# A transformer tower on one core: both feed-forward passes get another split of work between ScalarE, VectorE and GpSimd

## What is computed

```python
h = h + attention(layernorm(h))
x = layernorm(h)                                  # 32 x 257 tokens of 256 values
s = sigmoid(clip_x) * max(abs(x)) / 127           # one scale over all tokens
xq = clip(round(x / s), -128, 127) * s
gate, up = xq @ quant(w_gate).T, xq @ quant(w_up).T          # 704 wide
p = silu(gate) * up
s2 = sigmoid(clip_down) * max(abs(p)) / 127       # again over all tokens
hq = clip(round(p / s2), -128, 127) * s2
out = h + hq @ quant(w_down).T
```

## Time and profile before

| | us |
|---|---|
| median of 3 runs (lowest, highest) | 1266.56 (1261.84, 1271.71) |
| profiled execution, its own time | 1265.48 |
| its span, first to last instruction | 1263.6 |
| embedding, attention and preparation of weights, until about | 985 |
| first pass, first product to last maximum | 998.4 to 1129.3 |
| second pass, to the last residual addition | 1131.5 to 1260.0 |

### The profile page before, as it was taken

How to read it: one execution, slowest core, us unless ns; L and a number is a source line. 1 busy time by engine, 2 the same in 40 slices (tenths; PEclk the granted TensorE clock), 3 DMA queues, 4 the chain that set the end, 5 groups by cost and what they waited for, 6 DMA issues and landing times. The chain is left out here.

```text
span 1263.6 us, 27990 instructions
## 1 busy us (share of the span) xinstructions
PE 996.6 (79%) x9574; PEld 691.5 (55%) x9574; DVE 847.5 (67%) x1907; ACT 675.3 (53%) x1123; POOL 655.9 (52%) x749
## 2 busy tenths in 40 slices
PE   2257989999989998998989988897844577856785
PEld 1135766666766766666767766665633233323332
DVE  1125566677776777677776777665556388888985
ACT  0245655566666666566666666654321366655553
POOL 4235455556565565556555565643321799802333
PEclk9978899999999999999999999998876699987657
DMA  3565554555545655455545655333300144115653
GB/s 108 122 155 137 129 144 119 131 150 144 152 119 138 154 149 133 120 155 142 151 125 137 155 143 142 95 94 103 81 11 1 46 180 172 61 46 187 204 163 125
DMA packets 156710, 158.66 MB, mean 126 GB/s; under 512 B 28360, under 2 KB 152172, under 8 KB 154092
## 3 DMA queue, kind: packets, MB, share of 16 engines
q1 hardware_dynamic: 156652, 157.91, 46.3%
HBM read 70.38 MB, written 31.23 MB: 80 GB/s over the span
## 5 line engine op out<-in xcount | busy, mean ns | idle before, releaser
L518 ACT ACTIVATE prob<-ST 128x772 f32<-128x772 f32 x256 | 209.5, 818 | 165.6 <-PE ST L928 160.9
L683 DVE TENSOR_REDUCE mneg<-SX 128x2 f32<-128x258 f32 x256 | 107.5, 420 | 241.6 <-PE SX L914 241.2
L911 PE MATMUL SX<-kst,qst 96*128 96x257 bf16 (+1 forms) x1024 | 161.8, 252 | 25.5 <-DMA qst<-qpart 15.1
L685 DVE TENSOR_REDUCE mneg<-SX 128x2 f32<-128x514 f32 x256 | 173.9, 679 | 0.0
L928 PE MATMUL ST<-qst,kst 98*128 98x256 bf16 (+2 forms) x1536 | 139.9, 224 | 29.3 <-DMA qst<-mpart 29.1
L928 PEld LDWEIGHTS ST<-qst,kst 98*128 98x128 bf16 x1536 | 121.5, 100 | 48.3 <-issue 19.0
L914 PE MATMUL SX<-mask_s,ident_b 128*128 128x256 bf16 x512 | 143.5, 280 | 0.0
L444 POOL TENSOR_SCALAR_AFFINE_SELECT prob<-prob 128x1016 f32<-128x1016 f32 x128 | 142.6, 1114 | 0.0
L911 PEld LDWEIGHTS SX<-kst,qst 96*128 96x128 bf16 x1024 | 92.3, 99 | 71.9 <-issue 35.3
L947 PE MATMUL G<-prob,vaug 128*32 128x256 f32 (+2 forms) x3072 | 118.1, 283 | 9.3 <-POOL prob L444 8.6
L1553 PE MATMUL GU<-qst,hq 128*128 128x256 bf16 (+1 forms) x384 | 84.9, 371 | 46.0 <-ACT hq L1346 46.0
(11 more groups left out here) (236 smaller groups left out, 2152.4 us busy)
## 6 DMA issues: line engine op xcount, KB each, us to landing
kst<-kpart SPq DMA_DIRECT2D x192, 128.5 KB, 2.5
gst<-gray_dram SPq DMA_DIRECT2D x96, 256.0 KB
qst<-qpart SPq DMA_DIRECT2D x192, 128.0 KB, 2.4
h_dram<-hb SPq DMA_DIRECT2D x10, 1280.0 KB, 4.6
wg_raw<-in_x SPq DMA_DIRECT2D x48, 256.0 KB, 4.0
wu_raw<-in_x SPq DMA_DIRECT2D x48, 256.0 KB, 4.2
gray_dram<-gray SPq DMA_DIRECT2D x64, 128.0 KB, 2.9
hb<-h_dram SPq DMA_DIRECT2D x6, 1280.0 KB, 6.1
```

The lines of the kernel that those rows point to most:

```text
L518: nc.scalar.activation(prob[:, g % 2, 2 * (u % 2):2 * (u % 2) + 2, 0:QEND], ST[:, :, 0:QEND], ACT.Exp).then_inc(exp_done, 1)
L683: nc.vector.tensor_reduce(mneg[:, 0, u // 4, 0, at], SX[:, :, S0:S0 + P + 1], AX.X, ALU.max, negate=True)
L685: nc.vector.tensor_reduce(mneg[:, 1, u // 4, 0, at], SX[:, :, S1:S1 + T], AX.X, ALU.max, negate=True).then_inc(max_done, 1)
L911: mm(SX[:, r, at:at + k], qst[par][0:SR, 2 * u + r, P * t:P * t + P], kst[par][0:SR, 2 * u + r, 0:k], start=t == 1, stop=False)
```

## The change

In the first pass there are four silu buffers instead of two, counted on across blocks; the maximum is taken over one chunk at a time, one product behind; ScalarE normalises tiles 0 and 1 of each block (behind silu 0 and silu 2) and GpSimd only tiles 2 and 3. For this VectorE computes `nbias` = -mean x rstd once. In the second pass ScalarE scales three chunks and VectorE three; VectorE adds the residual in place of GpSimd, behind its L1472 pair. The last chunk of `wdT` is filled with zeros in partitions 64 to 127, and the matmuls of the second pass take all 128 rows in every chunk.

```diff
-        silu = work[:, 2:4, :]
+        NSI = 4
+        silu = work[:, 2:2 + NSI, :]
...
-        A2 = 2
+        A2 = 3
...
-            for i, w in enumerate([work] + hb + hkept):
+            for i, w in enumerate([wdT] + hb + hkept):
                 pool.wait_ge(s_pad, i + 1)
                 nc.gpsimd.memset(w[IW[-1]:P, IT - 1, :], 0.0).then_inc(s_pad, 1)
...
                     waitb(pool, xq_t, n - 2, 1, 1)
-                    for t in range(TT):
+                    for t in range(2, TT):
                         i = tile_of(n, t, 1)
                         nc.gpsimd.tensor_scalar(xn[par][:, t, :], h2f[:, tile_of(n, t, D)], mean2[:, i], rstd2[:, i],
                                                 ALU.subtract, ALU.mult).then_inc(xnorm, 1)
-                    waitb(pool, xnorm, n, TT, TT)
+                    waitb(pool, xnorm, n, TT - 2, TT - 2)
+                    waitb(pool, xnorm_act, n, 2, 2)
...
-            def add(n, par):
-                if on(n - 2):
-                    b = at2(n - 2)
-                    waitb(pool, oscaled, n - 2, 2, 2)
-                    o = oy[par][:, :, :].rearrange("p t d -> p (t d)")
-                    rows = slice(b * TT * D, (b + 1) * TT * D)
-                    nc.gpsimd.tensor_tensor(o, o, h2f[:, rows], ALU.add).then_inc(oy_ready, 1)
...
+            def normalise(b, par, t):
+
+                if on(b):
+                    if b == 0:
+                        act.wait_ge(c_step, 7)
+                    waitb(act, xq_t, b - 2, 1, 1)
+                    i = tile_of(b, t, 1)
+                    nc.scalar.activation(xn[par][:, t, :], h2f[:, tile_of(b, t, D)], ACT.Identity,
+                                         bias=nbias[:, i], scale=rstd2[:, i]).then_inc(xnorm_act, 1)
...
-                        if k >= 2:
-                            waitb(act, prod_done, bG, IT, k - 1)
-                        else:
-                            waitb(act, prod_done, bG - 1, IT, IT - 1 + k)
-                        nc.scalar.activation(silu[0:IW[k], k % 2, :], GU[k % 3][0:IW[k], 0, :], ACT.Silu,
+                        j = IT * bG + k
+                        if j >= NSI:
+                            act.wait_ge(prod_done, j - NSI + 1)
+                        nc.scalar.activation(silu[0:IW[k], j % NSI, :], GU[k % 3][0:IW[k], 0, :], ACT.Silu,
                                              scale=gsc[0:IW[k], k:k + 1]).then_inc(silu_done, 1)
+                        if k in (0, 2):
+                            normalise(n, par, k // 2)
                         if k == 4:
                             place_x(bT, 1 - par)
                 else:
+                    for t in range(2):
+                        normalise(n, par, t)
                     place_x(bT, 1 - par)
...
-            go(c_step, nc.vector.memset(amx[:, :], 0.0))
+            go(c_step, nc.vector.scalar_tensor_tensor(nbias[:, :], mean2[:, :], -1.0, rstd2[:, :],
+                                                      ALU.mult, ALU.mult))
...
+                    def largest(k):
+
+                        waitb(dve, prod_done, b, IT, k + 1)
+                        if b == 0 and k == IT - 1:
+                            dve.wait_ge(s_pad, 1 + 3 + NB - NR)
+                        last = nc.vector.tensor_reduce(pmax[:, b:b + 1, k:k + 1], h[:, k:k + 1, :], AX.X, ALU.max,
+                                                       apply_absolute_value=True)
+                        if k == IT - 1:
+                            last.then_inc(pmax_done, 1)
...
-                        nc.vector.tensor_tensor(h[0:IW[k], k, :], silu[0:IW[k], k % 2, :],
+                        nc.vector.tensor_tensor(h[0:IW[k], k, :], silu[0:IW[k], (IT * b + k) % NSI, :],
                                                 GU[k % 3][0:IW[k], 1, :], ALU.mult).then_inc(prod_done, 1)
-                        if k == 2:
-                            waitb(dve, prod_done, b, IT, 3)
-                            nc.vector.tensor_reduce(pmax[:, b:b + 1, 0:3], h[:, 0:3, :], AX.X, ALU.max,
-                                                    apply_absolute_value=True)
-                    waitb(dve, prod_done, b, IT, IT)
-                    if b == 0:
-                        dve.wait_ge(s_pad, 1 + 3 + NB - NR)
-                    nc.vector.tensor_reduce(pmax[:, b:b + 1, 3:IT], h[:, 3:IT, :], AX.X,
-                                            ALU.max, apply_absolute_value=True).then_inc(pmax_done, 1)
+                        if k >= 1:
+                            largest(k - 1)
+                    largest(IT - 1)
+
...
+                    b = ORDER[m]
+                    o = oy[par][:, :, :].rearrange("p t d -> p (t d)")
+                    waitb(dve, oscaled, m, 2, 2)
+                    nc.vector.tensor_tensor(o, o, h2f[:, b * TT * D:(b + 1) * TT * D], ALU.add).then_inc(oy_ready, 1)
...
-                                last = mm(GU[i][:, par, D * t:D * t + D], hq[par][0:IW[k], k, tok:tok + P],
-                                          wdT[0:IW[k], k, :], start=k == 0, stop=k == IT - 1)
+                                last = mm(GU[i][:, par, D * t:D * t + D], hq[par][:, k, tok:tok + P],
+                                          wdT[:, k, :], start=k == 0, stop=k == IT - 1)
```

More of the change, by code:

```diff
@@ L1110, in vit_tower @@
         gsc, usc, hsc = sb("gsc", [P, IT]), sb("usc", [P, IT]), sb("hsc", [P, IT])
+        nbias = sb("nbias", [P, B * QT])
         NC = B
@@ L1134, in vit_tower @@
         xnorm = sem("xnorm")
+        xnorm_act = sem("xnorm_act")
         xquant = sem("xquant")
@@ L1281, in _ @@
             nc.gpsimd.partition_all_reduce(gmx[:, 1:2], amx[:, 1:2], P, bass.bass_isa.ReduceOp.max).then_inc(c_pool, 1)
-            def add(n, par):
-                if on(n - 2):
-                    b = at2(n - 2)
-                    waitb(pool, oscaled, n - 2, 2, 2)
-                    o = oy[par][:, :, :].rearrange("p t d -> p (t d)")
-                    rows = slice(b * TT * D, (b + 1) * TT * D)
-                    nc.gpsimd.tensor_tensor(o, o, h2f[:, rows], ALU.add).then_inc(oy_ready, 1)
-            pipe2(pool, add)
         @block.scalar
@@ L1413, in first @@
                     h = h_of(b, par)
+                    def largest(k):
[6 more added lines that the diff above has]
+                            last.then_inc(pmax_done, 1)
+                    if 2 <= b < NR:
+                        dve.wait_ge(h_saved[par], 32 * (b // 2))
                     for k in range(IT):
                         waitb(dve, silu_done, b, IT, k + 1)
[L1416 to L1421, removed]
-                        nc.vector.tensor_tensor(h[0:IW[k], k, :], silu[0:IW[k], k % 2, :],
-                                                GU[k % 3][0:IW[k], 1, :], ALU.mult).then_inc(prod_done, 1)
-                        if k == 2:
-                            waitb(dve, prod_done, b, IT, 3)
-                            nc.vector.tensor_reduce(pmax[:, b:b + 1, 0:3], h[:, 0:3, :], AX.X, ALU.max,
-                                                    apply_absolute_value=True)
-                    waitb(dve, prod_done, b, IT, IT)
-                    if b == 0:
-                        dve.wait_ge(s_pad, 1 + 3 + NB - NR)
-                    nc.vector.tensor_reduce(pmax[:, b:b + 1, 3:IT], h[:, 3:IT, :], AX.X,
-                                            ALU.max, apply_absolute_value=True).then_inc(pmax_done, 1)
+                        nc.vector.tensor_tensor(h[0:IW[k], k, :], silu[0:IW[k], (IT * b + k) % NSI, :],
+                                                GU[k % 3][0:IW[k], 1, :], ALU.mult).then_inc(prod_done, 1)
+                        if k >= 1:
+                            largest(k - 1)
+                    largest(IT - 1)
             pipe(dve, first)
```

## The result

| | before | after |
|---|---|---|
| median of four runs each (lowest, highest), us | 1267.89 (1261.84, 1271.71) | 1233.96 (1229.39, 1235.22) |
| profiled execution: its own time, span | 1265.48, 1263.6 | 1229.39, 1227.7 |
| first VectorE instruction on `sg` (the sigmoids of the clip values) to the first product of the first pass | 30.9 | 28.4 |
| first pass, first product to the combining of the maxima | 130.9 | 120.8 |
| second pass, from there to the end of the last addition | 130.7 | 109.5 |

The ratio is 0.973, 95% interval 0.9683 to 0.9777: 34 us less, where 28 were forecast, and inside the forecast range of 1229 to 1249. Of the 35.9 us between the two spans, the three feed-forward stages give 2.5 + 10.1 + 21.2 = 33.8; the other 2.1 lie ahead of them, where the change does nothing: the first instruction on `sg` stands at 967.5 us before and at 965.3 after.

The account below looks back on a forecast made before the run. Closed loops through several engines, none full, were taken to bound both passes. Savings of 11.9 (first pass), 0.7 (head), 11.3 (13 positions) and 3.9 (last position) sum to 27.8 us, giving 1238.8, say 1239; range 1229 to 1249.

Parts of the forecast that it names:

- the loop becomes 8.12 - 0.59 = 7.53: First pass, per block: short maxima leave 1.79 us behind product 5 instead of 2.38, so the period falls to 7.53.
- Silu buffers: priced 0: First pass: the loop goes through PSUM buffers, so four silu buffers shorten nothing in it, 0 us.
- normalising hidden: First pass: ScalarE's two normalised tiles per block are hidden by waits for chunks, with as little as 0.1 us to spare.
- Priced at 1.25 on the loop: Second pass: VectorE's residual addition takes 1.25 us on the loop of two positions.
- 0.80 per position taken: Second pass matmuls: 128 rows throughout remove four row changes, 0.80 us per position, leaving 5.29 at half clock.
- 4.7 us for the last 24 matmuls: Second pass, last position: its matmuls take 4.7 us of a sum of about 12.65, which was 16.58 before.
- 0.4 off 5.29: Second pass, first position of a pair: TensorE's clock rising late saves 0.4 us of 5.29, from between 0 and 1.3.
- the four parts named there: Second-pass head: third ScalarE chunk costs 0.7, addition 1.2; matmuls give 0.8, L1477 falls from 3.06 to about 0.9.
- VectorE as the bound of the second pass: Rival, second pass: TensorE gets full clock throughout, so VectorE bounds at 5.5 us per position; 1225 us; 8%.
- ScalarE did not come to the first-pass path: Rival, first pass: normalised tiles delay silu 1 or 3, 0.5 to 1.0 us per block; 1247 to 1255 us; 13%.
- The clock did not fall in the first pass: Rival, first pass: TensorE falls to 1.2 GHz, adding 4.5 us per block, 72 in all; 1311 us; 2%.
- The loads did come late once: Rival, second pass: ScalarE waits for loads, a microsecond at a few of ten; 1242 us; 7%.

Follow-up runs that it names:

- r4: Changed kernel with the two long maxima over three chunks put back in the first pass; median 1244.86 us.
- r8: Kernel before with only the short maxima, one behind each product; 1253.53 us (one run).
- r9: Changed kernel with two silu buffers instead of four; 1235.78 us (one run).
- r10: Changed kernel with GpSimd normalising all four tiles of each block and ScalarE none; 1240.87 us (one run).
- r5: Changed kernel with the next block's transposes moved from behind chunk 3 to behind chunk 2 in the first pass; median 1232.88 us.
- r3: Changed kernel with GpSimd instead of VectorE adding the residual in the second pass; median 1237.95 us.
- r1: The changed kernel, unedited, measured once more in another set of runs; median 1232.30 us, ratio 0.977 to before.

## Why the prediction was right

**The first-pass loop.** The step "the loop becomes 8.12 - 0.59 = 7.53" measured 7.53, and r4 and r8 show that the maxima alone do it. "Silu buffers: priced 0" and "normalising hidden" hold (r9, r10). The start gave 2.5 us for 2.4, and r10 ties it to GpSimd's two tiles. The first pass gave 10.1 for the 9.5 that the sum had without the start. The difference is in the first block, 6.39 us from product 0 to product 5 where it was 6.87 before, and is TensorE's clock, as in r10; r8, with the short maxima alone, has 6.87 too. The floor of 7.14 under the loop is what r5 runs at.

**The addition on VectorE.** Priced at 1.25 on the loop; measured, with the 0.59 of the second half's scaling ahead of it (L1483), 1.87 us (1181.48 to 1183.35) for a forecast 1.84. Its removal from GpSimd also freed the scaling, 3.76 to 1.26 with one chunk fewer, and r3 shows the blocking by putting it back.

**The filled rows.** 0.80 per position taken; 0.79 and 0.73 measured. The trace is with the rule of TensorEngine Tiling (Array Packing), Key Properties, of the Trainium skill, that a change of tiling mode drains the engine; it shows that the time goes ahead of the 64-row loads, not that a drain is what it is. The row of the Trainium skill's TensorE: Matmul & The Clock Gate that gives few rows the same time holds for the matmul alone (353 ns in the mean for 64 rows against 374 for 128 in before's groups), and would mislead here, where the cost lies between matmuls.

**The terms that were too small.** The second pass gave 21.2 us for 15.9. Three terms make that up.

- The last position: 12.65 forecast, 10.86 measured. The term that failed is 4.7 us for the last 24 matmuls; they took 2.89.
- The 13 positions: 84.0 forecast with the class tokens, 81.4 measured. The term that failed is "0.4 off 5.29" for the first position of a pair: the six among them took 4.28, 4.24, 5.30, 5.30, 4.10 and 4.41, in the mean 4.60 instead of 4.89, 1.7 us in all. Another 0.9 is counting: 13 positions from one scaling to another hold six whole pairs and one short position of 5.5, not six and a half pairs.
- The head: 1.5 us gained for 0.7. Part of that is arithmetic: the four parts named there (0.7 and 1.2 lost, 0.8 and 2.2 gained) add to 1.1, not 0.7. They measured 0.7 lost, with a wait of VectorE of 1.04 for ScalarE ahead of the first clipping, 1.3 lost, 1.4 gained and 2.1 gained. The term that failed is the matmuls: from the start of the first 24 to the VectorE instruction that waits for their end it was 5.8 us before and 4.5 after.

Most of it is one thing: TensorE had more of its full clock than was taken, 1.8 us in the last position, 1.7 in the 13 and 0.6 in the head. r1 has the same second pass to 0.1 us, so this was no luck of one execution; but how far the clock would rise was an estimate between 0 and 1.3 us per pair that no row decided.

**The rivals.** VectorE as the bound of the second pass did not come about in the changed kernel; every second position still waits for the matmuls, by 1.80 us at half clock. ScalarE did not come to the first-pass path: r10, without its two tiles per block, has the same period of 7.53. The clock did not fall in the first pass: it was 0.99 over the stage. The loads did come late once:

```profile
1208.35 2.23 ACT L1348 ACTIVATE work<-work,magic,hsc 128x512 f32<-128x512 f32 x3 [1.57 <-DMA work<-h_dram]
...
1209.01 1.76 DVE L1473 TENSOR_SCALAR hb<-hb 128x3072 f32<-128x3072 f32 x1
1210.69 1.28 DVE L1483 TENSOR_TENSOR wu_raw<-GU,sd_row 128x512 f32<-128x512 f32 x2
1210.80 2.76 ACT L1354 ACTIVATE hq<-hb 128x3072 bf16<-128x3072 f32 x1 [0.23 <-DVE hb L1473]
```

ScalarE waited 1.57 us for the last block's load and was still 0.23 early for the conversion, so it cost nothing; there are 0.23 us left until it does.

## What to carry to other kernels

Where no engine is full, add up one period from an instruction to its next occurrence through all engines; only what stands on that loop is worth moving, and work that grows in sum (six short maxima for two long ones) can still shorten it if less stands behind its last link. The parts of this change look alike in the diff and were worth 9.5 us (maxima), 2.4 us (normalising), nothing (silu buffers) and 21 us (second pass, where undoing the addition, the third chunk or the filled rows costs 9.3, 5.6 or 4.8 in one execution each, a part of it clock). Once a loop is known, the next edit is known too: moving the transposes by one chunk and the addition behind the next clipping took 13 us more out of the feed-forward stages.

## What was not expected of the hardware

- The same second-pass code took 109.3 to 109.9 us in five executions (changed kernel, r1, r5, r9, r10) and 112.4 in r4; before's code took 127.6, 128.8 and 130.7. What differs is where within a burst of 24 matmuls the clock rises: bursts of the changed kernel took between 4.10 and 5.30 us for the first of a pair. So a stage that an edit ahead of it does not touch came out 3 us longer (r4), and the price of an edit should be read burst by burst and not from the stage's length. That r4's edit is the cause is not shown: before's own code, unedited, gave 130.7 and 128.8. What decides it in each case stays open; no run here varied only the time at which the stage begins.
- How late a load may be was closer than foreseen: 0.23 us.
